# A quantised feed-forward stage of a decoder, rewritten as one block

## The chip, the cores and the metric

One core of a Trainium2 chip runs the kernel. The metric is the device time of one launch in microseconds (us), and the median of the runs is compared.

## The reference

Four decoder layers run one after the other on x, 8 x 256 tokens of 128 features. Each layer adds self-attention, cross-attention and a feed-forward part, each of the layer norm of x. The change touches only the feed-forward part of the third layer, in which weights and activations are rounded to 8-bit steps:

```python
def _act_fake_quant(x, clip_factor):
    scale = jax.nn.sigmoid(clip_factor) * jnp.max(jnp.abs(x)) / QMAX
    return jnp.clip(_ste_round(x / scale), -QMAX - 1.0, QMAX) * scale
def _weight_fake_quant(w):
    scale = jnp.max(jnp.abs(w), axis=1, keepdims=True) / QMAX
    return jnp.clip(_ste_round(w / scale), -QMAX - 1.0, QMAX) * scale
xq = _act_fake_quant(x, clip_x[0])
gate = jnp.einsum('bsh,ih->bsi', xq, _weight_fake_quant(w_gate))
up = jnp.einsum('bsh,ih->bsi', xq, _weight_fake_quant(w_up))
h = _act_fake_quant(jax.nn.silu(gate) * up, clip_down[0])
return jnp.einsum('bsi,hi->bsh', h, _weight_fake_quant(w_down))
```

QMAX is 127. The scale of an activation comes from the maximum over the whole tensor, so nothing can be rounded before all of it is known: once for x, and once for h. w_gate and w_up are 352 x 128, w_down is 128 x 352.

## The kernel before, in words

x stays in SBUF as `c.xT`, 128 features on the partitions by T = 2048 tokens, in NTI = 4 tiles of NT = 512. The stages of the decoder follow one another, each made of one or more `nc.Block()`s: within a Block each engine has its own list of instructions, in the order written and tied by semaphores, and all engines meet at its end. So what an engine could do ahead of a Block's end waits for it.

`quantised_ffn` (L2690 on) is six Blocks:

1. SyncE alone issues the loads of the three weight matrices (`w`, 576 KB, L2746) and of the clip factors (L2747).
2. `layer_norm` (L319 on, shared by several stages) writes `c.xn`. Per tile: TensorE multiplies by 1/128 (`mean`, L223), VectorE subtracts (`centre`, L254), ScalarE squares (L243), TensorE sums (L205), ScalarE takes the root (`deviation`, L248), VectorE inverts (`invert`, L260), TensorE spreads the result (`spread`, L205) and VectorE multiplies (`scale`, L269).
3. VectorE takes the maximum of x (L2760) and of the weight rows (L2763, L2765), scales, clips and rounds the weights by adding and subtracting MAGIC = 1.5 * 2^23 (L2773 to L2778), does the same to x in three passes per tile (L2783 to L2785), and copies the turned weights out of PSUM (L2788). The maximum over partitions goes by TensorE: a transpose of the column into one row (L2737), a maximum on one partition (L2729), and a matmul that spreads it again (L2739).
4. Gate and up, U = 3 units (128 of the 384 padded inner rows) for each of 4 tiles, 12 in all: TensorE L2813 and L2814, ScalarE's Silu L2822, VectorE's product L2833, and behind each product the maximum of its 512 columns, L2836. The first tile is written out, the other three are a hardware loop (`tiles`).
5. The scale of h from these 12 maxima (L2846 on).
6. The down projection, again first tile and loop: ScalarE scales and rounds h (L2864), VectorE clips (L2874), GpSimd subtracts MAGIC into bf16 `hq` (L2885), TensorE multiplies into one PSUM bank (L2895), and VectorE adds the result to x (`residual`, L2877) at the end of each tile. VectorE's clips of the next tile are behind that, so all wait for the tile's last matmul.

The next stage, self-attention, begins with its own norm, on the same lines L223 to L269.

Of the kernel before, what the change touches and what calls it, by code (L numbers as in the profile page):

```python
# [29 lines left out]
P = 128  # L30
B, S, SC, D = 8, 256, 512, 128
T = B * S
# [2659 lines left out]
def quantised_ffn(c):  # L2692
# [4 lines left out]
    cv = Carver(c)  # L2697
    NB = len(QB)
    h = cv.f32(NB, T)
    w = cv.f32(3, NB * P)  # L2700
    clip = cv.f32(2)
    wr = cv.f32(3, NB * P)
    wq = cv.bf16(3, NB * P)
    wT = cv.bf16(3, NB * P)
    xq = cv.bf16(T)
    hq = cv.bf16(NB, T)
    sm = c.small
    wmax = sm[:, 0:7]
    wscale, wrec = sm[:, 8:15], sm[:, 16:23]
    sig = sm[:, 24:26]  # L2710
    amax, top, scale, rec = (sm[:, 32 + 4 * i:36 + 4 * i] for i in range(4))
    up_scale = sm[:, 64:70]
    down_scale = sm[:, 70:71]
    hmax = sm[:, 80:80 + NB * NTI]
    chain_n = [0]

    def linker(dve):
        def link(mm):

            chain_n[0] += 1  # L2720
            mm.then_inc(g["quant_chain"].sem, 1)
            dve.wait_ge(g["quant_chain"].sem, g["quant_chain"].at(chain_n[0]))
        return link

    def tensor_scale(dve, link, which):

        i = which
        dve.wait_ge(g["max_turned"].sem, g["max_turned"].at(i + 1))
        dve.tensor_reduce(top[0:1, i:i + 1], ps[0:1, 7, 0:P], X, ALU.max).then_inc(g["max_top"].sem, 1)  # L2729
        dve.wait_ge(g["max_spread"].sem, g["max_spread"].at(i + 1))  # L2730
        link(dve.tensor_scalar(scale[:, i:i + 1], ps[:, 7, 0:1], sig[:, i:i + 1], 1.0 / 127, ALU.mult, ALU.mult))
        link(dve.reciprocal(rec[:, i:i + 1], scale[:, i:i + 1]))

    def spread_max(pe, which, ready, n):

        pe.wait_ge(ready.sem, ready.at(n))
# [4 lines left out]
    ones = cv.f32(P)[0:1, :]  # L2741
# [6 lines left out]
    layer_norm(c)  # L2748
    with nc.Block() as block:

        @block.scalar
        def _(act):
            act.wait_ge(g["weights_in"].sem, g["weights_in"].at(32))
            act.activation(sig, clip, ACT.Sigmoid).then_inc(g["clip_sig"].sem, 1)

        @block.vector
        def _(dve):
            link = linker(dve)
            dve.memset(ones, 1.0)
            dve.tensor_reduce(amax[:, 0:1], c.xn[:, :], X, ALU.max, apply_absolute_value=True).then_inc(g["x_max"].sem, 1)  # L2760
            dve.wait_ge(g["weights_in"].sem, g["weights_in"].at(32))
            for i in range(2):
                dve.tensor_reduce(wmax[:, NB * i:NB * (i + 1)], w[:, i, :].rearrange("p (a n) -> p a n", a=NB), X, ALU.max,  # L2763
                                  apply_absolute_value=True)
            link(dve.tensor_reduce(wmax[:, 2 * NB:2 * NB + 1], w[:, 2, :], X, ALU.max, apply_absolute_value=True))  # L2765
            link(dve.tensor_scalar(wscale, wmax, 1.0 / 127, 1e-30, ALU.mult, ALU.max))
            link(dve.reciprocal(wrec, wscale))
            dve.wait_ge(g["clip_sig"].sem, g["clip_sig"].at(1))
            tensor_scale(dve, link, 0)
            dve.tensor_scalar(up_scale, wscale[:, 0:6], scale[:, 0:1], None, ALU.mult)  # L2770

            for i in range(2):
                dve.tensor_tensor(wr[:, i, :].rearrange("p (a n) -> p a n", a=NB), w[:, i, :].rearrange("p (a n) -> p a n", a=NB),  # L2773
# [506 lines left out]
```

## Time and profile before

| | before |
|---|---|
| median of 3 runs | 1710.17 us |
| lowest, highest | 1706.46, 1714.75 us |
| the profiled execution's own time | 1705.87 us |
| its span, first to last instruction | 1704.2 us |
| mean granted TensorE clock | 0.925 of full speed |
| busy share of the span: TensorE, VectorE, ScalarE, GpSimd | 86%, 58%, 47%, 27% |

The times of the trace are microseconds from the start of the span. The profiled execution's own time is 1.7 us over its span: that is what lies around the instructions. Rows name an engine (PE is TensorE, PEld its weight load, DVE VectorE, ACT ScalarE, POOL GpSimd, SPq the DMA issues of SyncE), a line of the kernel, and the tiles written and read; `arena` is a large area from which a stage carves its tiles, `ps` the eight PSUM banks, `small` a small area for columns.

### The profile page before, as it was taken

What the parts mean: (1) busy time and instruction counts of PE and PEld (TensorE: products, weight loads), DVE (VectorE), ACT (ScalarE), POOL (GpSimd) and SP (SyncE); (2) the same over time, 40 slices, a digit from 0 to 9 for tenths busy, and PEclk for the clock granted to TensorE, in tenths of its full rate; (3) what the DMA queues carried; (4) which work ended last, traced back from release to release, by engine and by line L of the source; (5) the groups of instructions that cost most, each with busy time, mean ns of one, the idle gap of its engine ahead of it and who ended that gap; (6) DMA issues with size and microseconds to landing.
All of it is one profiled execution on the core that took longest, in us unless ns stands there. A gap on an engine that the chain in (4) does not pass through costs nothing. (4 is left out here: it accounts for less than half of the span.)

```text
span 1704.2 us, 30351 instructions
## 1 busy us (share of the span) xinstructions
PE 1467.2 (86%) x10747; PEld 736.8 (43%) x10747; DVE 996.6 (58%) x1947; ACT 797.7 (47%) x1480; POOL 455.2 (27%) x658
## 2 busy tenths in 40 slices
PE   7988999999899998679767899889737888878886
PEld 5767634444454444257433532222404333523354
DVE  5666588886252221546547578996374574557435
ACT  3454436677433334025330237778333465446536
POOL 7112300000014664410235220000004354235411
PEclk9999999999989999689887998999957899979888
DMA  2000452220200000001000163220001520342000
GB/s 97 1 0 0 141 173 81 53 47 15 94 20 1 0 0 1 1 25 31 6 6 1 58 204 118 57 56 15 15 1 50 174 67 20 100 155 62 20 17 25
DMA packets 82393, 85.45 MB, mean 50 GB/s; under 512 B 7244, under 2 KB 67916, under 8 KB 81772
## 3 DMA queue, kind: packets, MB, share of 16 engines
q1 hardware_dynamic: 82296, 84.18, 15.9%
q8 instruction: 57, 0.93, 0.2%
q14 instruction: 40, 0.33, 0.1%
HBM read 51.06 MB, written 32.51 MB: 49 GB/s over the span
## 5 line engine op out<-in xcount | busy, mean ns | idle before, releaser
L1282 ACT ACTIVATE arena<-ps 128x1024 f32<-128x1024 f32 x256 | 261.9, 1023 | 111.6 <-PE ps L1191 110.6
L1176 PE MATMUL ps<-k_stack,q_stack 49*128 49x512 bf16 x512 | 192.6, 387 | 15.1 <-DVE small L1306 13.1
L1191 PE MATMUL ps<-q_stack,k_stack 51*128 51x256 bf16 x1024 | 191.6, 275 | 0.4 <-ACT arena L1282 0.4
L1303 DVE CUSTOM_DVE_ANT_0 small<-ps,mask_b 128x512 bf16<-128x512 f32 x256 | 168.0, 689 | 33.7 <-PE ps L1176 32.3
L1306 DVE TENSOR_REDUCE small<-ps 128x1 f32<-128x512 f32 x256 | 162.3, 685 | 22.1 <-PE ps L1176 21.0
L1492 DVE TENSOR_REDUCE small<-ps 128x6 f32<-128x768 f32 x128 | 122.6, 958 | 77.7 <-PE ps L1374 75.9
L1203 PE MATMUL ps<-arena,v_pad 128*32 128x256 f32 x2048 | 163.6, 394 | 1.1 <-ACT arena L1282 1.1
L1468 ACT ACTIVATE arena<-ps 128x384 f32<-128x384 f32 x256 | 117.8, 488 | 78.1 <-PE ps L1393 77.3
L1076 POOL TENSOR_SCALAR_AFFINE_SELECT arena<-arena 128x256 f32<-128x256 f32 x256 | 101.9, 406 | 86.2 <-ACT arena L1468 85.7
L2607 POOL TENSOR_TENSOR arena<-arena 128x512 f32<-128x512 f32 x64 | 79.6, 1265 | 99.1 <-ACT arena L2501 99.1
L2533 DVE TENSOR_TENSOR arena<-ps,arena 128x512 f32<-128x512 f32 x64 | 44.3, 692 | 101.0 <-PE ps L2448 100.9
L1183 PE MATMUL ps<-mask_b,ident_b 64*128 64x512 bf16 x512 | 99.9, 383 | 0.5
L1049 POOL TENSOR_TENSOR small<-small 128x16 bf16<-128x16 f32 x64 | 13.8, 216 | 310.8 <-DVE small L1309 286.4
L1176 PEld LDWEIGHTS ps<-k_stack,q_stack 49*128 49x128 bf16 x512 | 47.8, 94 | 113.1 <-DVE small L1306 82.2
L1191 PEld LDWEIGHTS ps<-q_stack,k_stack 51*128 51x128 bf16 x1024 | 75.6, 95 | 29.2 <-issue 6.8
L2495 ACT ACTIVATE arena<-ps 128x512 f32<-128x512 f32 x64 | 38.2, 597 | 89.9 <-PE ps L2444 89.9
L945 POOL TENSOR_TENSOR arena<-arena 128x512 bf16<-128x512 f32 x40 | 45.6, 1157 | 109.1 <-ACT arena L852 109.1
L223 PE MATMUL ps<-xT,mean_w 128*128 128x512 f32 x96 | 52.3, 696 | 21.1 <-DMA xT<-in_xT 4.7
L238 ACT ACT_TABLE_LOAD x14 | 18.0, 1283 | 112.1 <-PEq L1569 26.2
L2473 PE MATMUL ps<-arena 128*128 128x512 f32 x128 | 66.1, 602 | 0.7
L2444 PE MATMUL ps<-xn,arena 128*128 128x512 f32 x128 | 66.5, 602 | 0.0
L2448 PE MATMUL ps<-xn,arena 128*128 128x512 f32 x128 | 66.0, 598 | 0.0
(352 smaller groups left out, 3027.8 us busy)
## 6 DMA issues: line engine op xcount, KB each, us to landing
q_stack<-q_scratch SPq DMA_DIRECT2D x128, 96.0 KB
k_stack<-k_scratch SPq DMA_DIRECT2D x64, 192.0 KB
k_scratch<-arena SPq DMA_DIRECT2D x8, 768.0 KB, 4.1
k_stack<-k_scratch SPq DMA_DIRECT2D x64, 96.0 KB
q_scratch<-arena SPq DMA_DIRECT2D x4, 1152.0 KB, 5.7
arena<-in_ctxT SPq DMA_DIRECT2D x8, 512.0 KB, 5.9
k_scratch<-arena SPq DMA_DIRECT2D x8, 512.0 KB, 4.7
k_scratch<-arena SPq DMA_DIRECT2D x16, 256.0 KB, 4.5
```

Of the source, the lines that this page charges most:

```text
L1076: pool.affine_select(diag, diag, [[0, 2], [1, P]], ALU.is_ge, 0.0, 0, -1).then_inc(g["masked"].sem, 1)
L1176: pe.matmul(ps[:, t, :], c.q_stack[par][64 * e:64 * e + ROW_MAX, pr, t * P:(t + 1) * P], c.k_stack[par][64 * e:64 * e + ROW_MAX, pr, :], s ...
L1183: return pe.matmul(ps[:, 2 + 2 * (i % 2) + half, :], c.ident_b[r, :], c.mask_b[r, m:m + 2 * S], start=first, stop=False, skip_group_check= ...
L1191: mm = pe.matmul(ps[:, bank, (ch % 2) * S:(ch % 2 + 1) * S], c.k_stack[prv][64 * e:64 * e + ROWS, pr, ch * P:(ch + 1) * P], c.q_stack[prv] ...
L1203: mm = pe.matmul(ps[32 * j:32 * j + 32, 6 + grp % 2, 0:S], c.v_pad[par][:, piece, head_of(i), :], buf.probs[i % 8][:, piece * S:(piece + 1 ...
L1282: act.activation(buf.probs[i % 8], ps[:, bank:bank + 2, :].rearrange("p a n -> p (a n)"), ACT.Exp, scale=scale).then_inc(g["probs"].sem, 1)
L1303: dve.tensor_tensor_reduce(buf.junk[t], ps[:, t, :], c.mask_b[:, M_X + t * SC:M_X + (t + 1) * SC], 1.0, FLOOR, op0=ALU.add, op1=ALU.max, a ...
L1306: dve.tensor_reduce(out, ps[:, t, :], X, ALU.max).then_inc(g["maxed"].sem, 1)
L1468: act.activation(buf.probs[i % 8][:, 0:3 * P], ps[:, 4 + i % 2, 0:3 * P], ACT.Exp, scale=scale)\
L1492: dve.tensor_reduce(buf.m3[par][:, hf, :, pr % HALF, :], ps[:, bank:bank + 2, 0:3 * P].rearrange("p e (a n) -> p e a n", a=3), X, ALU.max)\
L2444: pe.matmul(ps[:, 2 + u % 2, :], w13[:, (ex * 4 + j) * P:(ex * 4 + j + 1) * P], x, start=True, stop=True)\
L2607: pool.tensor_tensor(slot(v), slot(v), share_e[v // 2 % 2], ALU.mult).then_inc(g["act_made"].sem, 1)
```

## The change

All six Blocks become one, and nothing of the stage is in a loop any more. In it:

- The weights' maxima are taken by VectorE between the steps of the norm, ScalarE scales and rounds the weights (`round_weights`), GpSimd clips them and subtracts MAGIC, and TensorE turns them behind the norm.
- The maximum of x is taken for tile 0 and for the other three apart. TensorE turns the column spread over 128 columns (`to_broadcast`), so each partition gets all 128 values and takes the maximum itself: no spreading matmul.
- x is scaled and rounded by ScalarE (`round_x`), clipped below and lowered by MAGIC into bf16 by VectorE (`lift_x`), and clipped above in bf16 (`top_x`). Tiles 2 and 3 are done between gate units. Six matmuls with no use for their result stand before the gate (`keep_clock`).
- The maxima of h are taken for three units at once (`tile_max`), the last tile's as two and one.
- In the down part ScalarE rounds as before; VectorE's `lift` clips below, subtracts and writes bf16; `top_h` clips above in bf16, for a tile's first unit on GpSimd, for the other two on VectorE. Each tile has its own PSUM bank, and its residual stands behind the next tile's units.

```diff
@@ quantised_ffn @@
     cv = Carver(c)
+    norm = Norm(c, cv)
...
-    layer_norm(c)
...
+            norm_pe(norm, pe)
+            turn_weights_of(0)
+            turn_weights_of(1)
+            spread_max(0, 2)
+            turn_weights_of(2)
+            keep_clock(c, pe, 6, bank=0)
+            pe.wait_ge(g["weights_kept"].sem, g["weights_kept"].at(2))
+            for u in range(N):
+                gate_up(u)
...
+            for t in range(NTI):
+                down(t)
...
-        pe.transpose(ps[0:1, 7, 0:P], amax[:, which:which + 1], c.ident[:, :]).then_inc(g["max_turned"].sem, 1)
-        pe.wait_ge(g["max_top"].sem, g["max_top"].at(which + 1))
-        pe.matmul(ps[:, 7, 0:1], ones, top[0:1, which:which + 1], start=True, stop=True).then_inc(g["max_spread"].sem, 1)
+                    mm = pe.transpose(ps[:, 7, k * P:(k + 1) * P], amax[:, col + k:col + k + 1].to_broadcast([P, P]), c.ident[:, :])
...
+            round_weights(0)
+            norm.deviation(act, 3)
+            round_weights(1)
+            round_weights(2)
...
             act.activation(sig, clip, ACT.Sigmoid).then_inc(g["clip_sig"].sem, 1)
+            act.activation(c.small[:, NT:NT + 1], c.consts[:, C_EPS:C_EPS + 1], ACT.Silu)
+            act.wait_ge(g["scaled"].sem, g["scaled"].at(1))
+            round_x(0)
+            round_x(1)
+            act.wait_ge(g["turned"].sem, g["turned"].at(3))
+            act.activation(part(wT, 2), ps[:, 6, :].bitcast(BF16)[:, 0:NB * P], ACT.Identity).then_inc(g["w_down_kept"].sem, 1)
+            for u in range(N):
+                if u in (0, U):
+                    round_x(2 + u // U)
+                silu(u)
...
+            for t in range(3):
+                norm.centre(dve, t)
             dve.wait_ge(g["weights_in"].sem, g["weights_in"].at(32))
...
+                dve.tensor_scalar(norm.tile(xq, t), norm.tile(xr, t), MAGIC - 128.0, MAGIC, ALU.max, ALU.subtract)\
...
+                dve.tensor_scalar(norm.tile(xq, t), norm.tile(xq, t), 127.0, None, ALU.min).then_inc(g["quantised"].sem, 1)
...
+                dve.tensor_reduce(hmax[:, col:col + 1], h[:, n0:n1, t * NT:(t + 1) * NT], mybir.AxisListType.XY, ALU.max, apply_absolute_value=True)\
...
             for t in range(NTI):
...
                 for n in range(U):
+                    lift(t * U + n)
+                    if n > 1:
+                        top_h(t * U + n - 1)
+                top_h(t * U + U - 1)
+                if t:
+                    residual(t - 1)
...
+                pool.tensor_scalar(part(wr, i), part(wr, i), MAGIC - 128.0, MAGIC + 127.0, ALU.max, ALU.min).then_inc(g["made"].sem, 1)
...
+                pool.tensor_scalar(part(wq, i), part(wr, i), MAGIC, None, ALU.subtract).then_inc(g["w_quant"].sem, 1)
+            for t in range(NTI):
+                pool.wait_ge(g["lifted"].sem, g["lifted"].at(NTI + t * U + 1))
+                pool.tensor_scalar(unit(hq, t * U), unit(hq, t * U), 127.0, None, ALU.min).then_inc(g["h_topped"].sem, 1)
```

How the instructions move, at three places. First VectorE in the norm of this stage; L254, L260 and L269 are the norm's steps, the rows with + are new line numbers (L2836 and L2838 the weights' maxima, L2905 the maximum of tile 0), those with - the lines of before:

```order
 L254 TENSOR_TENSOR arena<-xT,ps 128x512 x3
+L2836 TENSOR_REDUCE small<-arena 128x3
 L260 RECIPROCAL small<-small 128x4
 L254 TENSOR_TENSOR arena<-xT,ps 128x512
-L260 RECIPROCAL small<-small 128x4 x2
-L269 TENSOR_TENSOR xn<-arena,ps 128x512
+L260 RECIPROCAL small<-small 128x4
+L2836 TENSOR_REDUCE small<-arena 128x3
+L2838 TENSOR_REDUCE small<-arena 128x1
+L2896 TENSOR_SCALAR small<-small 128x7
+L2897 RECIPROCAL small<-small 128x7
+L260 RECIPROCAL small<-small 128x4
```

Five instructions on the weights now stand between the norm's third centring and its third inverse.

Then VectorE in the gate part, after the change (L2865 the product, L2870 the maximum, L2854 and L2859 the two passes over tile 3 of x):

```order
+L2865 SCALAR_TENSOR_TENSOR arena<-ps,small,arena 128x512 x3
+L2870 TENSOR_REDUCE small<-arena 128x1
+L2854 TENSOR_SCALAR arena<-arena 128x512
+L2859 TENSOR_SCALAR arena<-arena 128x512
+L2865 SCALAR_TENSOR_TENSOR arena<-ps,small,arena 128x512 x3
+L2870 TENSOR_REDUCE small<-arena 128x1
+L2865 SCALAR_TENSOR_TENSOR arena<-ps,small,arena 128x512 x3
+L2870 TENSOR_REDUCE small<-arena 128x1
+L2865 SCALAR_TENSOR_TENSOR arena<-ps,small,arena 128x512 x2
+L2870 TENSOR_REDUCE small<-arena 128x1 x2
```

One maximum follows three products, where one followed each; two passes over x stand among them.

Last ScalarE from the norm's end to the first Silus (L2788 and L2790 round the weights, L2794 rounds x, L2817 copies the turned down weights, L2799 is the Silu):

```order
+L2788 ACTIVATE arena<-arena,consts,small 128x128 x3
+L2790 ACTIVATE arena<-arena,consts,small 128x384
+L2811 ACT_TABLE_LOAD
+L2811 ACTIVATE small<-arena 128x2
+L2812 ACT_TABLE_LOAD
+L2812 ACTIVATE small<-consts 128x1
+L2794 ACTIVATE arena<-xn,consts,small 128x512 x2
+L2817 ACTIVATE arena<-ps 128x384
+L2794 ACTIVATE arena<-xn,consts,small 128x512
+L2799 ACTIVATE arena<-ps,small 128x512 x3
```

Both table loads now stand ahead of the rounding of x, and the first Silu stands behind three roundings and a copy.

## Rows read from the trace of the kernel before

**Rows 1.** Stretches of time: busy time of each engine, granted clock, DMA share.
```profile
core 0: us, PE busy (x) PEld busy (x) DVE busy (x) ACT busy (x) POOL busy (x), PEclk, DMA share, GB/s
1218.70:1232.00 13.30, 12.51 (x72) 9.33 (x72) 5.83 (x12) 4.87 (x10) 0.00 (x0) 0.87 0.12 41
1232.00:1248.00 16.00, 2.00 (x12) 1.45 (x12) 14.28 (x32) 1.49 (x2) 0.00 (x0) 0.63 0.01 1
1248.00:1268.00 20.00, 12.03 (x24) 1.94 (x24) 16.32 (x24) 9.31 (x13) 0.00 (x0) 0.50 0.00 0
1270.70:1293.40 22.70, 7.28 (x12) 1.26 (x12) 9.62 (x16) 8.57 (x12) 12.95 (x12) 0.50 0.00 0
...
1293.70:1704.20 410.50, 343.31 (x3220) 168.37 (x3220) 224.57 (x419) 211.39 (x524) 151.16 (x364) 0.91 0.22 72
```

**Rows 2.** Timeline from the stage's first issue to the norm's end (start us, us).
```profile
1217.46 0.36 SPq L2746 DMA_DIRECT2D arena<-in_w_quant  x1
...
1218.74 5.37 PE L223 MATMUL ps<-xT,mean_w 128*128 128x512 f32 x8 [2.35 <-PEq L2742]
...
1223.29 0.69 DVE L254 TENSOR_TENSOR arena<-xT,ps 128x512 f32<-128x512 f32 x1 [0.56 <-PE ps L223]
...
1225.23 0.18 DVE L260 RECIPROCAL small<-small 128x4 f32<-128x4 f32 x1 [1.25 <-ACT small L248]
...
1231.29 0.69 DVE L269 TENSOR_TENSOR xn<-arena,ps 128x512 f32<-128x512 f32 x1 [0.20 <-PE ps L205]
```

**Rows 3.** DMA issues of this stretch: size and time to landing.
```profile
arena<-in_w_quant SPq DMA_DIRECT2D x1, 576.0 KB, 3.4
```

**Rows 4.** Groups of instructions of the third Block: busy us, mean ns of one.
```profile
L2760 DVE TENSOR_REDUCE small<-xn 128x1 f32<-128x2048 f32 x1 | 2.2, 2215 | 0.0
...
L2784 DVE TENSOR_SCALAR arena<-arena 128x512 f32<-128x512 f32 x4 | 1.7, 427 | 0.1
...
L2765 DVE TENSOR_REDUCE small<-arena 128x1 f32<-128x384 f32 x1 | 0.5, 530 | 0.0
```

**Rows 5.** Timeline: the table load of the Sigmoid, and the fourth Block's start.
```profile
1232.26 1.28 ACT L2754 ACT_TABLE_LOAD   x1 [2.60 <-PEq L328]
...
1233.56 0.20 ACT L2754 ACTIVATE small<-arena 128x2 f32<-128x2 f32 x1
...
1248.16 0.59 PE L2813 MATMUL ps<-arena 128*128 128x512 bf16 x1 [5.17 <-PEq L2749]
...
1249.42 1.84 ACT L2822 ACTIVATE arena<-ps,small 128x512 f32<-128x512 f32 x3
...
1250.14 0.75 DVE L2833 SCALAR_TENSOR_TENSOR arena<-ps,small,arena 128x512 f32<-128x512 f32 x1 [2.28 <-ACT arena L2822]
```

**Rows 6.** Groups of the gate part.
```profile
L2833 DVE SCALAR_TENSOR_TENSOR arena<-ps,small,arena 128x512 f32 x9 | 6.7, 743 | 0.0
...
L2836 DVE TENSOR_REDUCE small<-arena x9 | 6.2, 686 | 1.3
```

**Rows 7.** Timeline: last maximum, scale of h, start of the down part.
```profile
1267.18 0.69 DVE L2836 TENSOR_REDUCE small<-arena  x1
...
1268.84 0.28 DVE L2729 TENSOR_REDUCE small<-ps 1x1 f32<-1x128 f32 x1 [0.46 <-PE ps L2737]
...
1270.76 8.57 ACT L2864 ACTIVATE arena<-arena,consts,small 128x512 f32<-128x512 f32 x12 [6.69 <-PEq L2841]
```

**Rows 8.** Single instructions of the down part (durations ns min/median/max), and who waits.
```profile
L2874 DVE TENSOR_SCALAR arena<-arena x12: 414/420/1279, 1271.6 to 1288.6; - x9, 128x512 f32<-128x512 f32 x3
...
DVE xT L2877 <- PE ps L2895: 11.9, 4, 3.8
```

**Rows 9.** Timeline: the next stage's first matmuls.
```profile
1293.71 5.67 PE L223 MATMUL ps<-xT,mean_w 128*128 128x512 f32 x8 [1.20 <-PEq L2856]
```

**Rows 10.** GpSimd with one input, elsewhere in the kernel.
```profile
L3077 POOL TENSOR_SCALAR arena<-arena 128x768 f32<-128x768 int32 x1 | 0.8, 832 | 7.8 <-DMA arena<-in_qscales 7.8
...
L1069 POOL COPY v_pad<-arena 128x512 f32<-128x512 f32 x4 | 2.4, 609 | 0.1
```

More of the change, by code:

```diff
@@ L2751, in _, with round_weights @@
         @block.scalar
         def _(act):
+            def round_weights(i):
+                act.wait_ge(g["w_scaled"].sem, g["w_scaled"].at(1))
+                if i < 2:
+                    for a in range(NB):
+                        s = slice(a * P, (a + 1) * P)
+                        mm = act.activation(wr[:, i, s], w[:, i, s], ACT.Identity, scale=wrec[:, NB * i + a:NB * i + a + 1], bias=magic)
+                else:
+                    mm = act.activation(part(wr, 2), part(w, 2), ACT.Identity, scale=wrec[:, 2 * NB:2 * NB + 1], bias=magic)
+                mm.then_inc(g["w_rounded"].sem, 1)
@@ new lines, in round_x, with silu @@
+            def round_x(t):
+                act.activation(norm.tile(xr, t), norm.tile(c.xn, t), ACT.Identity, scale=rec[:, 0:1], bias=magic)\
+                   .then_inc(g["rounded"].sem, 1)
+            def silu(u):
+                act.wait_ge(g["gate"].sem, g["gate"].at(u + 1))
+                act.activation(unit(h, u), ps[:, u % U, :], ACT.Silu, scale=up_scale[:, u % U:u % U + 1]).then_inc(g["silu"].sem, 1)
+            norm.preload(act)
+            for t in range(NTI):
+                norm.squares(act, t)
+                if t:
+                    norm.deviation(act, t - 1)
@@ new lines, in _ @@
+            lift_x(0)
+            top_x(0)
+            lift_x(1)
+            top_x(1)
+            for u in range(N):
+                if u in (1, U + 1):
+                    lift_x(2 + u // U)
+                    top_x(2 + u // U)
+                gated(u)
+                if u % U == 0 and u:
+                    tile_max(u // U - 1, u // U - 1, 0, U)
+                if u == N - 1:
+                    tile_max(NTI - 1, NTI - 1, 0, U - 1)
+                    tile_max(NTI, NTI - 1, U - 1, U)
@@ L2880, in _ @@
+            dve.wait_ge(g["scaled"].sem, g["scaled"].at(2))
+            residual(NTI - 1)
         @block.gpsimd
         def _(pool):
[L2882 to L2888 removed]
@@ L2889, in _ @@
-        def _(pe):
-            def body(t):
-                if not isinstance(t, int):
-                    pe.wait_ge(g["residual"].sem, g["residual"].at(t))
-                for n in range(U):
-                    pe.wait_ge(g["h_quant"].sem, g["h_quant"].at(t * U + n + 1))
-                    mm = pe.matmul(ps[:, 0, :], wT[:, 2, n * P:(n + 1) * P], hq[:, n, bass.ds(t * NT, NT)],
-                                   start=(n == 0), stop=(n == U - 1))
-                mm.then_inc(g["down"].sem, 1)
-            tiles(nc, ENG.PE, body)
@@ new lines, in _ @@
+            for t in range(NTI):
+                pool.wait_ge(g["lifted"].sem, g["lifted"].at(NTI + t * U + 1))
+                pool.tensor_scalar(unit(hq, t * U), unit(hq, t * U), 127.0, None, ALU.min).then_inc(g["h_topped"].sem, 1)
+    norm.advance()
+    g.advance(quant_chain=made[0], weights_in=32, w_scaled=1, w_rounded=3, made=3, w_quant=3, turned=3, weights_kept=2, w_down_kept=1,
+              clip_sig=1, x_max=3, max_turned=2, scaled=2, rounded=NTI + N, lifted=NTI + N, quantised=NTI + (U - 1) * NTI,
+              gate=N, up=N, silu=N, gated=N, h_max=NTI + 1, h_topped=NTI, down=NTI, residual=NTI)
```

262 lines of the change are left out of this document (123 added, 139 removed).

## The prediction

> **What bounds the kernel now.** I read the stretches of time first. TensorE is the busiest engine of the kernel as a whole, but not in this stage: behind its norm the engine that works most changes from stretch to stretch, VectorE 14.3 of 16 us, then 16.3 of 20 us, and then none, with GpSimd 12.95, VectorE 9.6 and ScalarE 8.6 of 22.7 us [rows 1]. All engines meet at each Block's end, so the stage's length is the sum of its parts: from the issue of the weights at 1217.46 [rows 2] to the next stage's first matmul at 1293.71 [rows 9], 76.25 us, 4.5% of the span. Its anchors in the timelines are: norm 1218.74 to 1231.98 [rows 2], the first gate matmul at 1248.16 [rows 5], the last maximum's end at 1267.87 and the first rounding of h at 1270.76 [rows 7], the next stage at 1293.71 [rows 9]. I cost the change against these five pieces.
>
> **The change, part by part.**
>
> *Start.* The block in which SyncE issues two loads holds all other engines from 1217.46 to 1218.74; in one Block the norm starts at 1217.5. **1.2 us saved.** The new wait for the weights stands on VectorE behind the third centring, and the norm's inverses, their spreading and every later step are queued behind it. The load lands 3.4 us after its issue [rows 3], at about 1220.9. Centring 3 ends at 1224.0 before [rows 2], now at 1222.7, so the wait costs nothing; the clip factors, issued 0.4 us later, have time too. The first maximum of weights (0.53 us, [rows 4]) lies in VectorE's idle time before the inverse [rows 2]. The others, some 1.4 us with their two small steps, end at about 1226.4, when the third inverse falls due at about 1226.6. Cover is thin here, so 0 to 0.7 us; I take 0. The maximum over tile 0 of x, 0.69 us, stands ahead of the last inverse, which would not be due before 1228.4.
>
> *From the norm's end to the first gate matmul, before 16.2 us.* The weights leave VectorE. ScalarE rounds them: 0.71 us per 512 columns when back to back [rows 7], so at 128 columns about 0.4 each, and some 3 us for all seven, in time in which it waited; only the fourth root stands behind three of them, and those end at 1227.8, before its input comes (1228.2, worked out as its time before less 1.2). GpSimd's six passes over 384 columns are about 0.5 us each by the nearest rows, 0.83 for 768 and 0.61 for 512 [rows 10], so the first two matrices are clean at 1228.9 and 1230.7, the third at 1231.8. VectorE needs only a maximum over 1536 columns (2.2 for 2048 [rows 4], so 1.7). What is left on the path behind the norm's end: 1.7 for that maximum, 0.8 for two wide transposes (before, one narrow one took 0.46 from the maximum's end to VectorE's start [rows 7]; 0.46 to 1.2), 0.85 for the maximum of 256 columns and two small steps, 0.8 for rounding tile 0 of x on ScalarE, 0.46 for the lift (0.43 for such a pass [rows 4], and a wait), and the bf16 minimum. No row has a VectorE pass that reads bf16 from SBUF: at most 0.43 like the f32 one, at least half; I take 0.3, as only the part that grows with the columns can halve. Sum 4.9, and 0.2 for waits: 5.1 against 16.2, **11.1 saved**. The six empty matmuls behind the last weight turn end at 1234.9 at 2.4 GHz or 1236.2 at 1.2 GHz, against the gate's 1235.8: 0 to 0.4 lost, and the first Silu waits for ScalarE's own queue till then.
>
> The two table loads are the other thing on this path. ScalarE reaches them at 1230.2; the load before the Sigmoid took 1.28 and its use came 1.30 after its start [rows 5], so both with their small uses end at 1233.1, 1.1 us before the scale of x is there. I price them at nothing. The Trainium skill, page "ScalarE: Activation LUTs", section "What ACT_TABLE_LOAD costs", adds a drain of 1.38 us to each load; the trace has none between load and use, and by that rule the rounding of x would start 1.7 us later.
>
> *Gate and up, before 19.7 us (1248.16 to 1267.87).* The first product came 2.0 us behind the first matmul, for a table load [rows 5]; now 1.6, as ScalarE copies the down weights and rounds tile 2 before the first Silu. From there VectorE sets the pace. Before: 12 products of 0.74 and 12 maxima of 0.69 [rows 6], 17.7 us with their waits. Now: 12 products at 0.68 start to start (8.2), three maxima of 1536 columns at 1.62 (4.9), one of 1024 and one of 512 (1.8), two lifts and two minima (1.4): 16.3. Sum 17.9, **1.8 saved**. ScalarE needs 0.61 per Silu [rows 5] and keeps ahead. A maximum reads its 1536 columns at one per cycle as it did, so what three units at once save is only the fixed part.
>
> *Scale of h, before 2.9 us.* No spreading matmul, no block ends, a slower wide transpose: 0.17 + 0.65 + 0.3 + 0.2 + 0.2 + 0.2 and waits, 1.9. **1.0 saved.**
>
> *Down, before 22.95 us (1270.76 to 1293.71).* VectorE waited 11.9 us in four waits for a tile's last matmul [rows 8], while its clips of the next tile, and GpSimd and TensorE after them, stood behind. Now ScalarE's twelve roundings, 8.6 us [rows 7], go through. VectorE has per tile three lifts (0.35 start to start), two minima (0.25) and a residual (0.66), 2.2 us against ScalarE's 2.14. Behind the last rounding come lift 0.45, minimum 0.3, matmul 0.6, residual 0.75, block end 0.3: 2.4. But a VectorE pass over SBUF doesn't run freely beside GpSimd: the same L2874 took 0.42 in the median and 1.28 at worst [rows 8]. GpSimd now has one pass per tile (0.6 us, [rows 10]), not three of 1.1; it starts when the first lift ends, and the second lift falls due about 0.35 us before it ends. I take 1.0 us over the four tiles, bounds 0 and 4 x 0.86 = 3.4. Sum 8.6 + 2.4 + 1.0 = 12.0, **10.95 saved**. The Trainium skill, page "SBUF — State Buffer", on the two sides of that memory, says that the two engines' shared ports are an exclusive lock for a whole instruction; by it a pass would wait for all that is left of GpSimd's, which is what 1.28 looks like.
>
> Total 1.2 + 11.1 + 1.8 + 1.0 + 10.95 = **26 us**. The profiled execution's own time, 1705.87 (span 1704.2 and 1.7 around it), becomes 1679.9. It lies 4.3 us under the median of the runs shown, 1710.17; the median of the changed kernel I put at 1710.17 - 26 = **1684 us**. By the bounds above the saving runs from 22 to 27.5. Clock changes come on top: the granted clock is 0.50, that is 1.2 GHz, from 1248 to 1293 [rows 1], behind long idle times of TensorE, and the first matmuls of the two norms take 5.37 and 5.67 us [rows 2, 9]. Wholly at 1.2 GHz these would be half at 2.4, so at most 2.8 us hang on it per norm.
>
> **The rivals.**
>
> 1. *VectorE and GpSimd block each other in the down part* (0.10). If every lift and minimum on VectorE took on average the 0.61 that the loop's L2874 took, 20 of them at 0.2 to 0.3 more: 4 to 6 us instead of 1. With the other bounds against it too (0.7, 0.4, 0.4, and 1.2 for the clock in a norm) the saving is about 18, at worst 15, and the time 1692 to 1695. For it: the 1.28. Against: GpSimd's work there falls from 12.95 to 2.4 us.
>
> 2. *The denser work raises TensorE's clock* (0.10). Its matmuls of the down part now stand in half the time, and the gate's behind six more. If it is up when both norms start, up to 5.5 us come on top, so a saving of 30 us or more, 1680 or less at the median. Against: the share of busy time stays well under that of the stages in which it is 0.9.
>
> 3. *Slower than before, by the clock behind the stage* (0.02). The 410.5 us that follow have the granted clock 0.91, and TensorE is busy for 343 of them [rows 1]. Shifted by 26 us, their work can meet other clock changes. The saving is gone when those stages take 6.3% longer, clock 0.855; at 0.82 they take 45 us longer and the kernel is at 1729. Against: the three runs with the same instructions differ by 8 us in all.
>
> 4. *Most of the saving fails* (0.04, within 0.5%, about 1706). The mechanism is the same clock at half the loss, or a wait in the norm: if the weights landed 5 us later, all of the norm would move with them, but nothing else is on the queues then.
>
> That the stage is covered by other work, so that nothing changes, I count under the fourth: each Block ends for all engines, so it is not.
>
> **How the numbers follow.** The forecast (saving 19 to 29 us) has 0.74, the rivals 0.10, 0.10, 0.02 and 0.04. A measurement of this kernel tells about 0.5%, 8.5 us, from no change. Faster by more: 0.74 + 0.10 + 0.10 = 0.94; same 0.04; slower 0.02. The range reaches from a saving of 32 us against the lowest run, 1674, to one of 15 against the median, 1695.
>
> **What the new profile would show.** The wait for the weights on VectorE is absent. The first gate matmul comes 18 us behind the stage's first issue, the first rounding of h 38, the next stage's first matmul 50. VectorE is without gaps between its first product and last maximum. In the down part ScalarE's twelve roundings are one row of 8.6 us, and VectorE's lifts are over 0.43 only where GpSimd runs. The forecast is wrong if the stage takes over 58 us, or if it takes 50 and the total still moves by under 18: then the stretches behind it changed.

## The result, and the profile after

| | before | after |
|---|---|---|
| median of the runs compared (4 and 4) | 1711.51 us | 1694.34 us |
| lowest, highest | 1706.46, 1714.75 | 1693.48, 1696.71 |
| ratio, 95% interval | | 0.9904, 0.9877 to 0.9932 |
| span of the profiled execution | 1704.2 | 1691.8 |
| from the stage's first issue to the next stage's first matmul | 76.25 | 53.5 |

The change makes the kernel faster by 17 us, where 26 were forecast; 1694.3 against 1684: just inside the range's upper end, 1695, and outside the saving of 19 to 29 us that the forecast stood for. The stage itself shrank by 22.7. First the stretches of the new profile, cut at the same places as in [rows 1]: norm, norm's end to first gate matmul, gate and up, down part, all behind the stage (busy time of each engine, granted clock, DMA share):

```profile
core 0: us, PE busy (x) PEld busy (x) DVE busy (x) ACT busy (x) POOL busy (x), PEclk, DMA share, GB/s
1224.10:1238.80 14.70, 14.20 (x76) 12.00 (x77) 8.38 (x18) 10.03 (x20) 5.35 (x4) 0.77 0.13 41
1238.80:1244.40 5.60, 3.54 (x15) 1.45 (x16) 4.54 (x11) 3.02 (x6) 2.67 (x2) 0.77 0.00 0
1244.40:1261.80 17.40, 8.21 (x25) 2.01 (x23) 15.97 (x22) 8.54 (x14) 0.00 (x0) 0.79 0.00 0
1263.60:1277.60 14.00, 5.89 (x12) 1.16 (x12) 11.60 (x24) 8.57 (x12) 6.48 (x4) 0.50 0.00 0
1277.60:1691.80 414.20, 349.92 (x3220) 169.88 (x3220) 224.67 (x419) 211.28 (x524) 151.22 (x364) 0.90 0.22 71
```

VectorE is now busy for 16.0 of 17.4 us in the gate part and 11.6 of 14.0 in the down part. GpSimd works 6.5 us in the down part where 2.4 were forecast, for four passes. The last stretch, the same instructions as before, took 414.2 us against 410.5.

The timeline of the anchors (start us, us), beside [rows 2], [rows 5], [rows 7] and [rows 9]:

```profile
1224.15 0.37 SPq L2727 DMA_DIRECT2D arena<-in_w_quant  x1
...
1224.19 3.67 PE L223 MATMUL ps<-xT,mean_w 128*128 128x512 f32 x8 [1.11 <-PEq L1811]
...
1238.10 0.69 DVE L269 TENSOR_TENSOR xn<-arena,ps 128x512 f32<-128x512 f32 x1 [1.02 <-PE ps L205]
...
1244.37 0.63 PE L2752 MATMUL ps<-arena 128*128 128x512 bf16 x1
...
1261.81 0.16 DVE L2929 TENSOR_REDUCE small<-small 128x1 f32<-128x5 f32 x1
...
1263.62 8.57 ACT L2824 ACTIVATE arena<-arena,consts,small 128x512 f32<-128x512 f32 x12 [6.47 <-DVE small L2931]
...
1277.68 6.18 PE L223 MATMUL ps<-xT,mean_w 128*128 128x512 f32 x8 [1.18 <-PEq L2723]
```

From the first issue the gate's first matmul comes after 20.2 us (forecast 18.4), the maximum over h after 37.7 (36.2), the first rounding of h after 39.5 (38.2) and the next stage after 53.5 (50.2). GpSimd's groups of this stage show three prices that bear on the first and the last of these four (busy us, mean ns of one):

```profile
L2952 POOL TENSOR_SCALAR arena<-arena 128x512 bf16<-128x512 bf16 x4 | 6.5, 1620 | 26.9 <-DVE arena L2876 26.9
L2947 POOL TENSOR_SCALAR arena<-arena 128x384 f32<-128x384 f32 x3 | 4.5, 1498 | 46.2 <-ACT arena L2788 46.1
L2949 POOL TENSOR_SCALAR arena<-arena 128x384 bf16<-128x384 f32 x3 | 3.5, 1178 | 0.2
```

1.50, 1.18 and 1.62 us, where the prediction took 0.5, 0.5 and 0.6 from [rows 10].

### The profile page after: what moved, and what is told of

It reads as the page before. It is cut to its first block and busy times, and to the rows that moved or that the text cites. A ratio compares the mean times of both kernels' runs of the same rounds, so it can differ in the third digit from the quotient of the medians.

```text
span 1691.8 us, 30123 instructions
## 1 busy us (share of the span) xinstructions
PE 1477.7 (87%) x10750; PEld 745.0 (44%) x10750; DVE 991.5 (59%) x1937; ACT 804.0 (48%) x1493; POOL 456.9 (27%) x656
## 5 line engine op out<-in xcount | busy, mean ns | idle before, releaser
L1176 PE MATMUL ps<-k_stack,q_stack 49*128 49x512 bf16 x512 | 193.3, 389 | 14.7 <-DVE small L1306 12.0
L1303 DVE CUSTOM_DVE_ANT_0 small<-ps,mask_b 128x512 bf16<-128x512 f32 x256 | 168.0, 689 | 33.7 <-PE ps L1176 32.4
L1306 DVE TENSOR_REDUCE small<-ps 128x1 f32<-128x512 f32 x256 | 162.3, 685 | 22.7 <-PE ps L1176 21.2
L1176 PEld LDWEIGHTS ps<-k_stack,q_stack 49*128 49x128 bf16 x512 | 47.8, 94 | 113.4 <-DVE small L1306 83.1
L2495 ACT ACTIVATE arena<-ps 128x512 f32<-128x512 f32 x64 | 38.2, 597 | 90.3 <-PE ps L2444 90.2
```

The costliest lines, as they stand in the source:

```text
L1176: pe.matmul(ps[:, t, :], c.q_stack[par][64 * e:64 * e + ROW_MAX, pr, t * P:(t + 1) * P], c.k_stack[par][64 * e:64 * e + ROW_MAX, pr, :], s ...
L1303: dve.tensor_tensor_reduce(buf.junk[t], ps[:, t, :], c.mask_b[:, M_X + t * SC:M_X + (t + 1) * SC], 1.0, FLOOR, op0=ALU.add, op1=ALU.max, a ...
L1306: dve.tensor_reduce(out, ps[:, t, :], X, ALU.max).then_inc(g["maxed"].sem, 1)
```

## The experiments

All times of the stage below are from its first issue, read in the run's own timeline. A single profiled execution carries the chance of the clock, so parts of the stage are compared, and totals only over several rounds.

**Both kernels once more.** What was expected of before:

> The kernel before, unchanged, profiled once more. The first profile of before and the one after the change differ by 4.6 us in the first 20 us of the program and by 5.5 us up to the stage, though the instructions there are the same. Theory 'chance of the clock': a second profile of before also has another start, 0 to 6 us longer than in the first profile (19.3 us from the first table load to the next one), and the time lies within 0.5% of before. Rival 'the change lengthens other stages': the stretch ahead of the stage is 1217 to 1218 us again, and only kernels with the change show 1223 to 1225.

Measured: 12 runs from 1701.91 to 1717.13 us, median 1710.95, ratio 0.9987 (0.9963 to 1.001). The first 20 us were as in the first profile (19.3 us), the low end of what was expected, but the later parts moved: the stage was reached at 1221.96 instead of 1217.46, with the kernel of before, so the rival fell. The stage took 77.6 us, as its norm ended 1.4 us later (granted clock 0.79, where it was 0.87), and the stretch behind it 414.3, where it was 410.5. Of the changed kernel:

> The changed kernel, unchanged, profiled once more. Both theories: the stage takes 53 to 54 us from its first issue to the next stage's first matmul, against 76.2 before. 'Chance of the clock': the stretches around it differ from the first profile by some us in either sign, the median of the difference over many rounds comes towards the stage's 22.7 us, 19 to 23. Rival 'the change lengthens other stages': the difference of the medians stays at 16 to 17.5 us, and the stretch behind the stage takes 413 to 415 us, not 410.

Measured: 1691.21 us, ratio 0.9884 (0.9849 to 0.9918), 20 us less than before's 1711.41. The stage took 53.7, and was reached at 1221.41, inside the spread of before. The stretch behind it took 412.3. So 'chance of the clock' has the difference inside its 19 to 23, and the rival, which wanted 16 to 17.5 and 413 to 415, has neither. The intervals of the two ratios overlap. The stage's 22.7 to 23.9 lies inside the second interval (14 to 26 us) and just above the first (12 to 21).

Where the first pair of profiles parts company is seen in the very first norm of the program, the same in both kernels. Before the change, then after it (timeline, the last 8 spreading matmuls of 128 columns, each in two passes):

```profile
16.59 2.03 PE L205 MATMUL ps<-ident,small 128*128 128x128 f32 x16
```

```profile
19.49 3.76 PE L205 MATMUL ps<-ident,small 128*128 128x128 f32 x16
```

Nearly twice the duration for the same work: the granted clock is 1.00 in one, that is 2.4 GHz, and 0.50, 1.2 GHz, in the other. The second table load came at 20.1 us in one and at 24.7 in the other. From the first table load to the second it was 19.3, 19.3, 23.9, 19.1, 17.6, 23.4, 22.3, 23.9, 22.0, 19.1, 19.1 and 26.6 us in the twelve profiles of this study (the first two are of before), in no order that follows the edits: the changed kernel alone has 23.9 and 19.1. Span less stage was 1627.9 and 1636.3 us in the two profiles of before, and 1638.3, 1633.7, 1635.0, 1633.2, 1634.8, 1639.8, 1638.8, 1632.1, 1630.3 and 1645.1 in those with the change. The profile on which I had worked, 1705.87 us in all, was the shortest of them outside the stage.

**The forms of a GpSimd pass.**

```diff
@@ quantised_ffn, gpsimd @@
+            for i, (dst, src, args) in enumerate(forms):
+                pool.tensor_scalar(dst, src, *args).then_inc(g["forms"].sem, 1)
+                pool.wait_ge(g["forms"].sem, g["forms"].at(3 + i))
```

> Nine more passes on GpSimd, over scratch, while it is idle in the gate part: 384 columns as multiply-add to f32 and to bf16, subtract to bf16 and to f32, add, minimum, maximum with minimum, then 512 bf16 columns as minimum and as multiply-add. Theory 'the operation sets the price': multiply-add over 384 takes 0.45 to 0.6 us as L3077 of before did per column (0.83 for 768), subtract about 1.2 and maximum with minimum 1.5 as in the weights, the bf16 minimum 1.5. Rival 'VectorE's port use sets it': all forms of a size take about the same here, where VectorE only does passes from PSUM and maxima. The whole takes 0 to 3 us more, as GpSimd's minimum of the first unit is not due until 21 us later.

The timeline of GpSimd, in the order given there: multiply-add to f32 and to bf16, subtract to bf16 and to f32, add, minimum, maximum with minimum, all over 384 columns, then the two passes over 512 bf16 columns (minimum, multiply-add):

```profile
1240.80 0.68 POOL L2966 TENSOR_SCALAR arena<-arena 128x384 f32<-128x384 f32 x1
...
1241.56 0.76 POOL L2966 TENSOR_SCALAR arena<-arena 128x384 bf16<-128x384 f32 x1
...
1242.40 1.17 POOL L2966 TENSOR_SCALAR arena<-arena 128x384 bf16<-128x384 f32 x1
...
1243.65 1.17 POOL L2966 TENSOR_SCALAR arena<-arena 128x384 f32<-128x384 f32 x1
...
1244.90 1.18 POOL L2966 TENSOR_SCALAR arena<-arena 128x384 f32<-128x384 f32 x1
...
1246.17 1.22 POOL L2966 TENSOR_SCALAR arena<-arena 128x384 f32<-128x384 f32 x1
...
1247.47 1.50 POOL L2966 TENSOR_SCALAR arena<-arena 128x384 f32<-128x384 f32 x1
...
1249.05 1.49 POOL L2966 TENSOR_SCALAR arena<-arena 128x512 bf16<-128x512 bf16 x1
...
1250.63 0.69 POOL L2966 TENSOR_SCALAR arena<-arena 128x512 bf16<-128x512 bf16 x1
```

With one input of the same size, a multiply followed by an add takes 0.68 to 0.76 us, subtract or add alone 1.17 to 1.18, the minimum 1.22, maximum with minimum 1.50, and over 512 bf16 columns the minimum 1.49 and the multiply-add 0.69. Each form ran once here; subtract and maximum with minimum cost what they cost in the weights, 1.18 and 1.50, where VectorE did other work. The operation sets the price, as expected; the 0.68 and 0.76 are somewhat over the 0.45 to 0.6 expected. Of the two rows that I took the price from [rows 10], L3077 is a multiply-add and the other a copy. The trace of before has two more one-input passes of this kind: L421, an add and a multiply, 3.92 us for 4480 columns, and a compare and a multiply:

```profile
L423 POOL TENSOR_SCALAR kmask_b<-arena 8x2048 bf16<-8x2048 int32 x1 | 7.1, 7092 | 0.1
```

That is 0.9 ns a column for the first and 3.5 for the second, where L3077 has 1.1. Their types differ too, so that spread is not by the operation alone, but it stood in the trace before the change. In the run with the nine passes the stage took 53.9 us, 0.2 more than in a_again, and this one execution 1690.63.

**The minimum of each tile's first unit on VectorE.**

```diff
@@ quantised_ffn, vector @@
                     lift(t * U + n)
+                    if n == 1:
+                        top_first(t)
@@ gpsimd @@
-            for t in range(NTI):
-                pool.wait_ge(g["lifted"].sem, g["lifted"].at(NTI + t * U + 1))
-                pool.tensor_scalar(unit(hq, t * U), unit(hq, t * U), 127.0, None, ALU.min).then_inc(g["h_topped"].sem, 1)
```

> The minimum of each tile's first unit goes from GpSimd to VectorE, so GpSimd does nothing in the down part. Theory 'GpSimd's passes and the shared ports set the 2.88 us of a tile': VectorE then needs 3 x 0.35 + 3 x 0.25 + 0.66 = 2.5 us per tile, no lift is over 0.45, and the down part takes 12.3 to 12.8 us instead of 14.0: 1 to 2 us less. Rival 'VectorE is the bound by its own work': one pass more for it, the tile takes 3.1 us and the down part 14.5 to 15.

The lifts (durations ns min/median/max) in the changed kernel, then here:

```profile
L2876 DVE TENSOR_SCALAR arena<-arena x12: 409/422/865, 1264.5 to 1273.5; 128x512 bf16<-128x512 f32 x12
```

```profile
L2876 DVE TENSOR_SCALAR arena<-arena x12: 417/422/429, 1260.9 to 1269.0; 128x512 bf16<-128x512 f32 x12
```

Without GpSimd no lift is over 0.43 us, and the down part took 11.8 us instead of 14.1: 2.3 less, somewhat more than expected, with one pass more on VectorE per tile; the rival (14.5 to 15) fell. Stage 51.5, total 1688.56, ratio 0.9862 (0.9829 to 0.9896), whose interval overlaps that of a_again. One tile of the changed kernel shows the coupling (timeline):

```profile
1269.94 1.49 DVE L2876 TENSOR_SCALAR arena<-arena 128x512 bf16<-128x512 f32 x3
...
1270.44 1.66 POOL L2952 TENSOR_SCALAR arena<-arena 128x512 bf16<-128x512 bf16 x1 [1.22 <-DVE arena L2876]
...
1271.36 0.89 DVE L2880 TENSOR_SCALAR arena<-arena 128x512 bf16<-128x512 bf16 x2
...
1272.16 1.46 PE L2763 MATMUL ps<-arena 128*128 128x512 bf16 x3 [1.42 <-POOL arena L2952]
...
1272.17 0.73 DVE L2885 SCALAR_TENSOR_TENSOR xT<-ps,small,xT 128x512 f32<-128x512 f32 x1
```

A tile takes 2.88 us from lift to lift, and VectorE has no gap in it, so its own passes set the pace: while GpSimd's runs, the three lifts (3 x 0.35 alone) and the two minima (0.49 alone) take 1.49 and 0.89. The tile's matmuls wait for GpSimd's pass, which ends at 1272.10, but VectorE does not wait for them before the last tile. The third lift and the first minimum by themselves (the same timeline in narrower windows):

```profile
1270.61 0.82 DVE L2876 TENSOR_SCALAR arena<-arena 128x512 bf16<-128x512 f32 x1
...
1271.36 0.28 DVE L2880 TENSOR_SCALAR arena<-arena 128x512 bf16<-128x512 bf16 x1
```

Both end while GpSimd's pass of 1.66 us still runs, the lift 0.4 us longer than alone and the minimum at its 0.28. The second minimum, to 1272.25, is again 0.4 longer. So in this tile GpSimd's pass costs two passes of VectorE 0.8 us together; it does not hold VectorE up for its whole length.

**The residual undone.**

```diff
@@ quantised_ffn, vector @@
-                if t:
-                    residual(t - 1)
-            dve.wait_ge(g["scaled"].sem, g["scaled"].at(2))
-            residual(NTI - 1)
+                if t == 0:
+                    dve.wait_ge(g["scaled"].sem, g["scaled"].at(2))
+                residual(t)
```

> One part undone: each residual directly behind its own tile's units, as before the change, all else as changed. If the residual a tile later is what removed the waits for the last matmul (11.9 us in four waits before), VectorE waits 0.7 to 1 us for TensorE in each of three more tiles and the down part takes 16 to 18 us instead of 14.0. Rival 'the gain of the down part comes from GpSimd doing 4 passes instead of 12': it stays at 14 to 14.7.

Measured: the down part took 18.75 us, 4.7 more than in the other profile of the same stage, and just over the range expected. The residuals' row in the groups of the down part says what VectorE waits for:

```profile
L2885 DVE SCALAR_TENSOR_TENSOR xT<-ps,small,xT 128x512 f32<-128x512 f32 x4 | 3.0, 751 | 5.2 <-PE ps L2763 5.2
```

5.2 us in four waits; 11.9 before the change [rows 8]. Of the 9 us that the down part gained, 4.7 need the residual a tile later. The rival, that all of the gain comes from GpSimd's fewer passes, fell; how the other 4 us divide between those and the rest of the part was not taken apart. The total of this one execution was 1699.92.

**The maxima undone.**

```diff
@@ quantised_ffn, vector @@
-                if u % U == 0 and u:
-                    tile_max(u // U - 1, u // U - 1, 0, U)
...
+                tile_max(u, u // U, u % U, u % U + 1)
```

> One part undone: a maximum for each unit, as before the change. By fixed parts (686 ns for 512 columns, 1740 for 1536, so 0.1 us saved in each of two) and one wait on the product just issued (0.1 to 0.15 each), the piece from the first gate matmul to the last maximum grows from 17.4 us by 1.5 to 2.5. Rival: VectorE waits for products anyway and it grows by less than 0.7.

Measured: from the first gate matmul to the last maximum 19.4 us, against 17.8 in a_again, whose norm ended at the same 11.6 us: 1.6 more, at the low end of what was expected. The maxima of three units are worth that much.

**Without the empty matmuls.**

```diff
@@ quantised_ffn, tensor @@
-            keep_clock(c, pe, 6, bank=0)
```

> The changed kernel without the six empty matmuls before the gate. Theory 'GpSimd's long weight passes push the empty matmuls in front of the gate': the gate's first matmul comes 0.3 to 0.6 us behind the second minimum of x tile 0, instead of 0.6 us behind it with TensorE busy up to it, and the piece from the norm's last product to the first gate matmul shrinks from 5.6 us by 0.4 to 0.6. Rival 'the empty matmuls keep the clock and pay': the gate's matmuls take 0.61 instead of 0.38 each, ScalarE's Silus wait for them, and the stage is longer by 0.5 to 1.

Measured: this profile lacks the record of the first gate matmul. The first on record, at 1242.02, is the up matmul L2755; the gate's weight load is there, and the first product can be compared. Without the empty matmuls, then in the changed kernel:

```profile
1241.20 0.29 DVE L2858 TENSOR_SCALAR arena<-arena 128x512 bf16<-128x512 bf16 x1
...
1241.61 0.10 PEld L2752 LDWEIGHTS ps<-arena 128*128 128x128 bf16 x1 [2.07 <-issue]
...
1243.03 0.75 DVE L2864 SCALAR_TENSOR_TENSOR arena<-ps,small,arena 128x512 f32<-128x512 f32 x1 [0.87 <-ACT arena L2798]
```

```profile
1245.76 0.75 DVE L2865 SCALAR_TENSOR_TENSOR arena<-ps,small,arena 128x512 f32<-128x512 f32 x1 [1.34 <-ACT arena L2799]
```

The norm ended at 1236.53 here and at 1238.79 there, so the first product comes 6.50 us behind it instead of 6.97: 0.47 earlier, inside the 0.4 to 0.6 expected, and the weight load stands 0.12 us behind the second minimum of tile 0. The theory holds: GpSimd's long weight passes push the empty matmuls in front of the gate. The rival fell: the gate's matmuls run at 1.2 GHz at first with and without them (0.63 us each), and the stage is 53.2 us against 53.5. Of the 0.47 only 0.15 is left at the stage's end, counted from the norm's. That is one execution, with a norm that ended late, as in the first profile; where it ends early they cost more, as the weight passes show below.

**GpSimd's weight passes made quick.** On top of top_dve; the kernel also leaves out the clip of the weights:

```diff
@@ quantised_ffn, gpsimd @@
-                pool.tensor_scalar(part(wr, i), part(wr, i), MAGIC - 128.0, MAGIC + 127.0, ALU.max, ALU.min).then_inc(g["made"].sem, 1)
-                pool.wait_ge(g["made"].sem, g["made"].at(i + 1))
-                pool.tensor_scalar(part(wq, i), part(wr, i), MAGIC, None, ALU.subtract).then_inc(g["w_quant"].sem, 1)
+                pool.tensor_scalar(part(wq, i), part(wr, i), 1.0, -MAGIC, ALU.mult, ALU.add).then_inc(g["w_quant"].sem, 1)
```

> top_dve, and GpSimd's two passes per weight matrix become one in the quick form (times 1, less MAGIC, 0.76 us for 384 columns); the clip of the weights is left out, since a weight divided by its row's maximum over 127 never leaves it. Theory 'GpSimd's weight passes stand on the path to the gate': the third matrix is turned 4 us earlier, the empty matmuls end before x is ready, and the gate starts 0.5 to 0.7 us earlier; the whole is 0.5 to 1 us shorter than top_dve and its stage takes 50.5 to 51.0. Rival 'they are covered': within 0.2 us of top_dve's stage, 51.4.

Measured: stage 47.8 us against 51.5 for top_dve, with the norm's end at 11.59 in both. The gate starts at 16.70 instead of 20.06. I had expected 0.5 to 0.7 and got 3.4. The timelines of the stretch show where. First a_again (which has the same gate as top_dve):

```profile
1234.55 1.18 POOL L2949 TENSOR_SCALAR arena<-arena 128x384 bf16<-128x384 f32 x1
...
1235.78 0.34 PE L2735 MATMUL ps<-ident_b,arena 128*128 128x128 bf16 x3 [2.50 <-POOL arena L2949]
...
1236.16 0.36 DVE L2849 COPY arena<-ps 128x384 bf16<-128x384 bf16 x1 [1.12 <-PE ps L2735]
...
1236.45 0.42 DVE L2843 TENSOR_REDUCE small<-ps 128x1 f32<-128x256 f32 x1
...
1238.88 0.29 DVE L2859 TENSOR_SCALAR arena<-arena 128x512 bf16<-128x512 bf16 x1
...
1239.34 2.34 PE L184 MATMUL ps<-mask_b,ident_b 128*128 128x512 bf16 x5 [0.22 <-DVE arena L2859]
...
1241.47 0.63 PE L2752 MATMUL ps<-arena 128*128 128x512 bf16 x1
```

Then lean_weights:

```profile
1231.41 1.11 POOL L2953 TENSOR_SCALAR arena<-arena 128x384 bf16<-128x384 f32 x2 [1.27 <-ACT arena L2788]
...
1234.20 0.61 DVE L2849 COPY arena<-ps 128x384 bf16<-128x384 bf16 x2
...
1234.88 0.43 DVE L2843 TENSOR_REDUCE small<-ps 128x1 f32<-128x256 f32 x1
...
1234.99 1.24 PE L184 MATMUL ps<-mask_b,ident_b 128*128 128x512 bf16 x5
...
1237.17 0.29 DVE L2859 TENSOR_SCALAR arena<-arena 128x512 bf16<-128x512 bf16 x1
...
1237.61 0.38 PE L2752 MATMUL ps<-arena 128*128 128x512 bf16 x1 [1.38 <-DVE arena L2859]
```

The second weight matrix is late from GpSimd, so TensorE turns it late, VectorE's copy of it waits, and behind that copy, in VectorE's order, stands the maximum that the scale of x comes from: VectorE waits 1.12 us for it, and tile 0 of x is ready 17.8 us behind the first issue instead of 16.6, 1.2 us later. The third matrix then holds the empty matmuls (L184) in front of the gate: five of the six are on record, at 1.2 GHz, and the gate comes 2.30 us behind the second minimum of tile 0, where it comes 0.15 behind it with quick passes: 2.15 us. With quick passes both are gone: the gate comes 5.11 us behind the norm's end. A pass here took 0.51 on average. The total was 1688.56 us, ratio 0.9858 (0.9828 to 0.9887), which is that of top_dve: the 3.7 us of the profiled stage don't show in it.

**That version again, and one that keeps TensorE busy.**

> lean_weights once more, beside warm_down and before on one chip. The stage takes 47.5 to 48.0 us from its first issue, or up to 49.5 if the clock falls within its norm; the ratio to before is 0.983 to 0.987, since 28.5 us of 1711 leave the stage (76.25 to 77.6 before) and the chance of the clock moves single runs by up to 10 us. Rival 'other stages give back 5 us': ratio 0.987 to 0.990.

Measured: 1685.06 us, ratio 0.9845 (0.9824 to 0.9867), as expected; but the profiled stage took 50.9, over my 49.5, since its norm ended at 14.7 instead of 11.6 with the clock down (0.54 in its second half, 1.00 in lean_weights). The gate again came 5.12 us behind the norm's end. Beside the changed kernel's first profile, whose norm ended as late, the quick passes save only 0.5 us up to the gate, and 3.4 beside a_again.

```diff
@@ quantised_ffn, tensor, on lean_weights @@
+            pe.wait_ge(g["gated"].sem, g["gated"].at(N - 1))
+            keep_clock(c, pe, 4, bank=4)
...
+                    if t < NTI - 1 or n < U - 1:
+                        keep_clock(c, pe, 1, bank=4, width=NT // 2)
```

> lean_weights with four empty matmuls behind the last product and one of 256 columns behind each down matmul, so that TensorE is busy up to the stage's end. Theory 'the 1.2 GHz in the down part is carried into the next stage' (its first 32.3 us had the granted clock 0.87 and took 2.1 us more than before the change): the next norm's first matmuls take 3.7 to 4.5 us instead of 6.1, the next stage's first part (table load to table load) takes 29.5 to 30.5 us instead of 32.3, and the time is 1.5 to 3 us under lean_again. Rival 'the fall comes at another time whatever TensorE does': that part stays at 32 to 32.7, or a later one grows by as much, and the time is within 1 us.

The next norm's first matmuls, lean_again and then warm_down (timeline):

```profile
1271.40 5.77 PE L223 MATMUL ps<-xT,mean_w 128*128 128x512 f32 x8 [1.18 <-PEq L2723]
```

```profile
1280.57 3.67 PE L223 MATMUL ps<-xT,mean_w 128*128 128x512 f32 x8 [1.18 <-PEq L2723]
```

They ran at 2.4 GHz throughout. The next stage's first part took 29.9 us against 30.3 in lean_again and 32.3 in lean_weights. The stage took 47.4 us. The total was 1683.62, ratio 0.9829 (0.9805 to 0.9853), 1.4 us under lean_again, just short of the 1.5 to 3 expected, and the intervals don't part the two. So the local gain is shown, and whether it reaches the end is not.

## Why the prediction came out as it did

**Two steps failed.** One is the price of GpSimd's passes, "about 0.5 us each by the nearest rows" and "0.6 us, [rows 10]": they took 1.50, 1.18 and 1.62, which cost 2 us in the down part and 0.5 to 3.4 before the gate. The other is that the stage's saving was taken off the median whole, with all that lies outside the stage put at no change: of the 22.7 us 17.2 arrived. Why those 5.5 did not stays open; what the runs show of it stands under the total.

- **Start, 1.2 saved: right.** The norm's first matmul comes 0.04 us behind the first issue, 1.28 before. The weights landed after 3.3 us.
- **The norm, no change: not so.** TensorE now idles 1.11 us before the norm instead of 2.35 [rows 2], and the norm's first eight matmuls took 3.67 us, at 2.4 GHz, in all ten profiles with the change; before they took 5.37 and 6.73. That is what the second rival had in mind, at this norm; no run takes the idle time by itself, so that it is the cause is not shown. In seven of the ten the norm then ended 11.6 us behind the first issue, 1.7 ahead of the 13.3 forecast; in three, the first profile among them (1.4 behind the forecast), the clock fell in its second half and it ended at 14.5 to 14.7.
- **The wait for the weights, nothing: right.** The norm's inverses were not late for it. The wait was not absent, as I had written it would be: VectorE idled 0.26 us for the small clip load.
- **Norm's end to the gate, 11.1 saved: the step that failed is the price of GpSimd's passes.** I wrote "about 0.5 us each by the nearest rows"; they took 1.50 and 1.18, so in a_again the three matrices were clean 2.8 us apart, not 1.8 and 1.1. The rest of the step was right: once GpSimd was quick, the gate came 5.11 us behind the norm's end, for 5.1 forecast. In the first profile of the change the clock fell in the norm's second half, so the norm ended at 14.6 us and 5.6 us remained; in a_again it ended at 11.6 and 8.5 remained. The gate started at 20.2 and 20.1, 1.7 to 1.8 us over the forecast, for different reasons: in the first profile 1.4 is the norm's late end and 0.5 the price of the passes (the empty matmuls behind the third matrix), and in a_again the price cost 3.4 and took back all that the norm had gained.
- **Gate and up, 1.8 saved: right, a little more came.** 17.4 and 17.8 against 17.9 forecast, before 19.7. The bf16 minimum took 0.29, my 0.3.
- **Scale of h: right.** 1.8 for 1.9.
- **Down, 10.95 saved: too much by 2.** 14.0 instead of 12.0. The mechanism was named, VectorE held up beside GpSimd, and its bounds of 0 to 3.4 held it; its size rested on a pass of 0.6 that took 1.62, again the price. Taken away, the part took 11.8; my sum without the 1.0 us and with four more minima of 0.25 would be 12.0, so I had the rest right to 0.2. The lengthened passes add up to 2.9 us over the four tiles. The first rival (VectorE and GpSimd slowing each other) was the true one in kind, though the part kept 9 of 11 us. The Trainium skill, page "SBUF — State Buffer", on the two sides of that memory, says that the shared ports are an exclusive lock for the whole instruction. The trace agrees in kind only: lifts took up to 0.865 us beside GpSimd and none over 0.429 without it, but VectorE passes start and end within one GpSimd pass of 1.66 us, and the two slowed ones lose 0.8 of it.
- **Table loads, nothing: right.** In a_again the second load's use ended at 1235.4, ahead of the scale of x at 1237.3. From the Sigmoid's load to its use it was 1.29 in the first profile of the change; the 1.38 us drain of the Trainium skill's page "ScalarE: Activation LUTs", section "What ACT_TABLE_LOAD costs", does not show.
- **Sum for the stage:** 26 forecast, 22.7 to 23.9 measured. With GpSimd quick it was 28.5 in one profile (47.8 against 76.25), whose norm ended at 11.6, and 25.4 in the next (50.9), whose norm ended at 14.7.
- **The total, 17 where the stage alone gave 22.7:** this part stays open. The profile of before was the luckiest of the study outside the stage, so comparing two profiles overstates what is lost elsewhere (10.3 us by the first pair). With more rounds the change is 20 us, and top_dve's total fell by 22.9 where its stage was 24.8 to 26.1 shorter. Behind the stage no loss shows: that stretch took 410.5 and 414.3 us before and 409.9 to 414.5 in the ten profiles with the change. Within it, the next stage's first part took 30.3 and 32.4 us before; with the change it took between 29.8 and 32.8, and 32.3 or more in seven of the nine profiles without warm_down. It follows the clock with which that norm starts: in all twelve profiles it took 30.3 or less where the norm's first eight matmuls took up to 5.77 us, and 32.3 or more where they took 6.07 or longer, before and after alike. Ahead of the stage, where all kernels run the same instructions, the stage was reached at 1217.5 and 1222.0 before and at 1220.4 to 1225.4 with the change (1233.1 in warm_down). Two profiles of before are too few to tell whether that is more than chance; it needs many of both kernels.

My range had no upper bound for GpSimd's price: both rows of [rows 10] were cheap forms. L423 would have given an upper one, 1.3 us for 384 columns and 1.8 for 512 at 3.5 ns each, an estimate across types. And a row with a subtraction was at hand in L2885 of before, with two inputs, at a mean of 1.07 to 1.11 us in the down part; it stands in the prediction's own text as what GpSimd is rid of. There I wrote that the lift of 1.28 us looks like a wait for all that is left of GpSimd's pass; the changed kernel's rows show no such whole wait.

## What to carry to other kernels

Price a pass by a row with the same operation, not only the same size and number of inputs; if there is none, take as the upper bound the dearest pass on that engine. Work moved to an idle engine is free only while it is not late and does not slow the engine beside it: look for the in-order queue in which someone waits for it, here VectorE's copy of the weights with the scale of x behind it, and the empty matmuls with the gate behind them. Read a saving of 1 to 2% in the stage's own timeline, and the total over many rounds, since the same instructions moved by up to 17 us between executions. Before a profile is taken as showing that an instruction starts late, look whether its record is there at all: the weight load and the next consumer tell.

## What the runs showed of the hardware

- A GpSimd pass with one input over 384 f32 columns took 0.51 to 0.76 us as multiply-add, 1.17 to 1.18 as subtraction or addition alone, 1.22 as minimum and 1.50 as maximum with minimum; over 512 bf16 columns 0.69 as multiply-add and 1.49 to 1.67 as minimum. The multiply by 1.0 makes a subtraction cheaper.
- The granted clock of the same instructions differed between executions: from the first table load to the second the program took 17.6 to 26.6 us.
- With 1.11 us of idle TensorE before the norm its first eight matmuls ran at 2.4 GHz (3.67 us) in ten profiles of ten; with 2.35 us they took 5.37 and 6.73 us, in part at 1.2 GHz.
- A VectorE pass that reads and writes bf16 over 512 columns took 0.28 us, its f32 to bf16 form 0.42. Beside a GpSimd pass of 1.66 us on bf16 two of VectorE's passes took 0.4 us longer each, and one between them took its usual 0.28.
